# A mixture-of-experts tile loop on one core: both first-product halves of a tile in a row, then the turn, then both output halves of the preceding tile

## What is computed

```python
xf = x.reshape(-1, C)                                   # 4096 tokens, C = 256
logits = jnp.einsum('nc,ec->ne', xf, router_w)          # 8 experts
top_w, top_i = jax.lax.top_k(jax.nn.softmax(logits, axis=-1), TOP_K)
top_w = top_w / jnp.sum(top_w, axis=-1, keepdims=True)
comb = jnp.einsum('nk,nke->ne', top_w, jax.nn.one_hot(top_i, E, dtype=xf.dtype))
h = jax.nn.gelu(jnp.einsum('nc,ech->enh', xf, w1), approximate=False)   # 1024 hidden
y = jnp.einsum('enh,ehc->enc', h, w2)
out = jnp.einsum('ne,enc->nc', comb, y)
```

## Time and profile before

| what | before |
|---|---|
| runs | 735.88, 734.77 and 732.49 us, median 734.77 us |
| profiled execution | 730.98 us, span 729.1 us, mean granted clock 0.901 |
| PE busy | 616.1 us, 84% of the span |
| DVE busy | 378.1 us, 52% |
| ACT busy | 344.4 us, 47% |
| POOL busy | 264.2 us, 36% |
| chain that ended last | PE 59%, issue 15%, POOL 13%, DVE 5%, ACT 5% |

### The profile page before, as it was taken

How to read it: one execution, slowest core, us unless ns; L and a number is a source line. 1 busy time by engine, 2 the same in 40 slices (tenths; PEclk the granted TensorE clock), 3 DMA queues, 4 the chain that set the end, 5 groups by cost and what they waited for, 6 DMA issues and landing times.

```text
span 729.1 us, 19000 instructions
## 1 busy us (share of the span) xinstructions
PE 616.1 (84%) x5885; PEld 487.5 (67%) x5885; DVE 378.1 (52%) x1132; ACT 344.4 (47%) x686; POOL 264.2 (36%) x198
## 2 busy tenths in 40 slices
PE   3792855933998899889997999999989999999994
PEld 3482555622776777578766867768777778778782
DVE  1565663576338544843484348556756444444441
ACT  3353434444353745363545355645543554554551
POOL 0104371243046324632363336442646322232222
PEclk9999555555899999989998999999999999999998
DMA  9996412122143333323333311432333523223222
GB/s 297 379 355 214 146 38 88 32 91 74 45 111 80 76 59 111 82 66 67 111 68 80 70 49 32 98 80 45 97 52 85 117 47 52 45 46 52 47 31 23
DMA packets 44233, 68.14 MB, mean 93 GB/s; under 512 B 4832, under 2 KB 35808, under 8 KB 44000
## 3 DMA queue, kind: packets, MB, share of 16 engines
q1 hardware_dynamic: 30848, 49.09, 21.4%
q0 software_dynamic: 13296, 17.83, 14.8%
HBM read 44.89 MB, written 23.35 MB: 94 GB/s over the span
## 4 chain that ended last, share of the span: by engine, by line
PE 59%; issue 15%; POOL 13%; DVE 5%; ACT 5%; DMA 2%; SPq 0%; POOLq 0%; DVEq 0%; ACTq 0%
PE bank L696 13%; PE bank L682 8%; PE bank L684 7%; PE bank L683 7%; PE bank L697 7%; POOL rows L1509 5%; PE bank L506 4%; POOL hrs L1496 3%; PE bank L587 2%; POOL out L1519 2%; PE bank L644 2%; PE bank L618 2%; PE bank L572 1%; PE bank L559 1%; POOL rs L1476 1%
## 5 line engine op out<-in xcount | busy, mean ns | idle before, releaser
L682 PE MATMUL bank<-xT,wall 128*128 128x128 f16 x1136 | 213.7, 223 | 19.5 <-ACT xT L892 15.3
L684 PE MATMUL bank<-xT,wall 128*128 128x128 f16 x1136 | 214.3, 223 | 0.0
L683 PE MATMUL bank<-xT,wall 128*128 128x128 f16 x1136 | 214.0, 223 | 0.0
L696 PE MATMUL bank<-wall,ffn 128*128 x568 | 197.2, 387 | 3.0 <-DVE yo L1295 3.0
L1519 POOL DMA_INDIRECT out<-yo,dst x71 | 115.7, 1629 | 194.7 <-DVE yo L1295 114.5
L884 ACT ACTIVATE ffn<-bank 128x512 f32<-128x512 f32 x142 | 84.7, 596 | 189.1 <-PE bank L684 188.2
L682 PEld LDWEIGHTS bank<-xT,wall 128*128 x1136 | 114.4, 101 | 40.2 <-issue 27.2
L1289 DVE TENSOR_TENSOR gl<-ffn 128x512 f16<-128x512 f32 x94 | 65.0, 691 | 136.9 <-ACT ffn L884 75.1
L684 PEld LDWEIGHTS bank<-xT,wall 128*128 x1136 | 113.3, 100 | 1.2
L683 PEld LDWEIGHTS bank<-xT,wall 128*128 x1136 | 113.3, 100 | 1.0
L697 PE MATMUL bank<-wall,gl 128*128 x376 | 103.9, 276 | 0.0
(11 more groups left out here) (139 smaller groups left out, 874.9 us busy)
## 6 DMA issues: line engine op xcount, KB each, us to landing
wall<-in_w SPq DMA_DIRECT2D x15, 1024.0 KB, 11.8
xrow<-rows SPq DMA_DIRECT2D x71, 130.0 KB, 2.1
xin<-in_x SPq DMA_DIRECT2D x8, 512.0 KB, 4.5
kT<-in_ctx_t SPq DMA_DIRECT2D x8, 512.0 KB, 4.4
ctn<-in_ctx SPq DMA_DIRECT2D x8, 512.0 KB, 4.7
xres<-in_x SPq DMA_DIRECT2D x8, 512.0 KB, 5.0
out<-xres SPq DMA_DIRECT2D x8, 512.0 KB, 3.1
rows<-in_const_pad SPq DMA_DIRECT2D x9, 130.0 KB, 9.1
```

What stands on the lines that cost most here:

```text
L682: pe.matmul(o, hi, xT[i % XT][:, c, :], start=(c == 0), stop=False)
L683: pe.matmul(o, hi, xT[i % XT][:, CK + c, :], start=False, stop=False)
L684: mm = pe.matmul(o, lo, xT[i % XT][:, c, :], start=False, stop=(c == CK - 1))
L696: pe.matmul(YB[:, :], gh[q][:, m4, :], weights(i, w, 2 * D), start=(a == 0 and m4 == 0), stop=False)
```

## The change

Three engines' orders are changed, and nothing else: no instruction of a tile is added or dropped, and no buffer or wait is changed. On PE `hidden(i, 1)` follows `hidden(i, 0)` at once, ahead of the turn; `output(i-1, 1)` then follows the slot's pieces without a first-product half between; the four `values` products of slot 0 stand together behind it. On ACT `gelu(i, 1)` follows `gelu(i, 0)`, ahead of `tile_high(i+1)` and the slot's pieces. On DVE `low(i, 1)` follows `low(i, 0)`, ahead of `tile_low(i+1)` and the slot's pieces.

```diff
@@ PE, step
                     if live(i):
                         hidden(i, 0)
+                        hidden(i, 1)
                     if live(i + 1):
                         tile_turn(i + 1)
...
                     if j == 7 and f is not None:
                         gates(f)
-                    if live(i):
-                        hidden(i, 1)
-                    if j == 0 and w is not None:
-                        values(w, 0)
-                        values(w, 1)
-                        values(w, 2)
                     if live(i - 1):
                         output(i - 1, 1)
                     if j == 0 and w is not None:
-                        values(w, 3)
+                        for b in range(G):
+                            values(w, b)
@@ ACT, step
                     if live(i):
                         gelu(i, 0)
+                        gelu(i, 1)
                     if j == 1 and w is not None:
                         values(w, 2)
...
-                    if live(i):
-                        gelu(i, 1)
                     if live(i - 1):
                         weigh(i - 1)
@@ DVE, step
                     if live(i):
                         low(i, 0)
+                        low(i, 1)
                     if j == 0 and m is not None:
                         log_forget(m)
...
-                    if live(i):
-                        low(i, 1)
                     if live(i - 1):
                         weigh(i - 1)
```

## The result

The changed kernel takes 851.94 us (median of 3 runs, 848.29 to 854.79) against 734.77: a ratio of 1.160 (95% interval 1.151 to 1.168). The prediction was 834 us, range 803 to 880. The profiled execution took 851.94 us with a span of 850.1, so 121.0 us of span were added where the prediction's sum had 99.4.

A forecast was written before the change was run, and what follows sets the result against it. The prediction took TensorE's own work to bound the kernel, nearly all of a plain tile's 5.76 us. Its terms, 48.4 + 5.0 + 22.0 + 24.0 = 99.4 us, gave 830.4 on the profiled run, 834 us as median; range 803 to 880.

The forecast's parts named there:

- The chain: Plain tile: from the first output half's last matmul through gelu, difference and turned rows to the next tile's first matmul, 2.40 us.
- the idle time: Plain tile: TensorE has 1.42 us of own work against 2.40 us, so it waits 1.0 us each tile.
- The slow pair: Plain tile: after a wait both first-product blocks run at the slow, queue-refilling rate, 3.78 us instead of about 2.7.
- Rival 1: First-product pairs: the second block regains its speed, 1.34 us instead of 1.89, total 810 us; chance 0.12.
- plain stretch: Last pass, tiles 44 to 70 without attention: 7.62 us a tile against 5.76, over 26 tiles +48.4 us.
- The clock in the last pass: TensorE's granted clock should stay 1.00 there in spite of the waits.
- rival 2: Waits in every tile make the clock fall: about 905 us, 870 if half the time; chance 0.11.
- Slot 0: First of a pass's eight tile-and-attention slots: second block delays scores and values by one block, +1.9 us each pass.
- Slots 1 and 3: Attention passes: VectorE's list steps and residual addition lengthen the wait for rows, +3.1 us and 8.76 us a tile.
- slots 2 to 4: Passes 3 to 5: an existing 5.10 us wait swallows the added time, leaving +0.6 us a pass at half clock.
- Slot 7: Last slot: +0.5 us in passes 6 and 7 for a half-queued second block, nothing in passes 3 to 5.
- slots 1 to 6: Passes 6 and 7: these six tiles take 48.6 us against 39.98, +8.6 us each pass.

The follow-up runs named there:

- e3: The changed kernel with four gelu and four difference buffers instead of three, row and output buffers two instead of three: 791.3 us.
- e5: The changed kernel with VectorE's order put back as before, TensorE and ScalarE still changed: 807.5 us.
- e9: The changed kernel with ScalarE's copy of the turned rows put between the two gelus, ahead of the second: 848.2 us.
- e1: The changed kernel with ScalarE's and VectorE's orders put back, so only TensorE's order differs from the kernel before: 737.5 us, ratio 1.0055.
- e4: The changed kernel with expert 0's weights at a fixed address for every tile, so no register work between matmuls: 769.7 us.

## Why the prediction held, and where it was short

**The chain** was right step by step: 2.40 us predicted, 2.41 measured. So was the idle time, 1.0 us a tile. e3, e5 and e9 show that the three buffers and the two orders make it.

**The slow pair** was right in kind: it is slow because it follows a wait while registers are worked out (e1 and e4). Rival 1, a second block that regains its speed, did not happen: from first to last matmul the first block takes 1.83 us on average and the second 1.78 (tiles 44 to 69). The size was short. In the mean of these tiles the pair takes 3.97 us to the turn, the turn 0.25, the output half 1.19 and the chain 2.42, together 7.83. So the pair is 0.19 us longer than the 3.78 charged, the chain 0.02, and the other two are as charged (the turn of 0.31 in tile 51 is an odd one). These 0.2 us make the 5.4 of the plain stretch. In tile 51 the pair shows some single gaps of 0.1 to 0.2 us beside the beat; what makes them was not tried.

**The clock in the last pass** was right: 0.99, so rival 2 did not happen there. In the passes with attention, where the sum took the clock of before but for 0.6 us behind slot 3's wait, it moved both ways: pass 3 fell from 0.98 to 0.88, passes 6 and 7 from 1.00 to 0.95 and 0.97, pass 5 from 0.93 to 0.92, and pass 4 rose from 0.93 to 0.96. Whether the waits did this is not shown: each figure is of one execution, executions of the kernel before stood anywhere from 0.87 to 0.94 in the mean at nearly the same time, and e5, whose tiles wait too, kept 1.00 through passes 6 and 7.

**Slot 0** is the step that failed in its reason. The prediction held that the values wait for the scores anyway and charged one block, 1.9 us. It overlooked VectorE: `scores` (L1054) now stands behind the second difference too. The slot in pass 3 of the changed kernel, VectorE and then TensorE:

```profile
214.10 0.69 DVE L1284 TENSOR_TENSOR gl<-ffn 128x512 f16<-128x512 f32 x1 [0.28 <-ACT ffn L882]
...
214.79 1.28 DVE L1054 SCALAR_TENSOR_TENSOR ct<-bank,ct 128x512 f32<-128x512 f32 x2
```

```profile
216.13 4.79 PE L587 MATMUL bank<-vt,ct 128*128 128x65 f32 x24 [1.38 <-DVE ct L1054]
```

and in pass 7:

```profile
544.20 2.89 PE L587 MATMUL bank<-vt,ct 128*128 128x65 f32 x24 [1.30 <-DVE ct L1054]
```

The values wait 1.3 to 1.4 us in each pass, 6.8 us in all, where before 1.5 us was lost. In passes 3, 5 and 6 the 24 products also take 4.79, 4.65 and 3.51 us for 2.89, part of them at a granted clock of 0.50. Slot 0 grew by 3.6, 1.7, 3.5, 2.4 and 1.9 us, 13.1 in all for 9.5 charged. e5 shows that VectorE's order makes most of it: with the second difference back behind the scores the values wait 0.3 to 0.4 us, here in pass 6,

```profile
450.31 2.89 PE L587 MATMUL bank<-vt,ct 128*128 128x65 f32 x24 [0.41 <-DVE ct L1054]
```

and slot 0 is only 3.2 us longer in all than before, though the second block stands ahead of the last decay product there too. So about a third of the 1.9 us charged for that block is paid in e5, and the rest of slot 0's growth is VectorE's.

**Slots 1 and 3** were right: +3.1 to +3.9 in slot 1 for 3.1; in passes 6 and 7 slot 3 takes 8.89 and 8.99 us for 8.76, and in passes 3 to 5 its long wait swallows what slot 2 adds, as the prediction said; slots 2 to 4 came out even there, for the 1.8 us charged in the three passes.

**Slot 7** was mis-sized: 0.5 us were charged in passes 6 and 7, and 1.8 and 1.7 came. The router's steps on VectorE stand behind the second difference there, and the ranks wait for them; in e5, where they stand ahead of it again, slot 7 grew by 0.6 and 0.7. In passes 3 to 5, where nothing was charged, it changed by 2.8, -1.0 and 0.1 us; the cause of these was not followed. VectorE in pass 6, and TensorE's wait:

```profile
526.76 0.69 DVE L1284 TENSOR_TENSOR gl<-ffn 128x512 f16<-128x512 f32 x1 [2.26 <-ACT ffn L882]
527.37 0.18 DVE L1135 TENSOR_TENSOR oh<-cst,km 128x32 f32<-128x32 f32 x1
...
530.05 0.19 DVE L1159 TENSOR_TENSOR msk<-oh 128x32 f16<-128x32 f32 x1
```

```profile
530.30 0.19 PE L627 MATMUL bank<-msk,cbf 128*128 128x32 f16 x1 [1.25 <-DVE msk L1159]
```

What is left of the 7.4 us in passes 6 and 7 lies in slots 1 to 6 (10.5 and 11.0 us for 8.6). Slot 6 took 8.50 and 8.48 us where 7.7 was charged, pass 7 had been 1.1 us shorter before (38.9) than pass 6, from which both charges were taken, and the pair's missing 0.2 us a tile is part of the rest. How much of each pass is the lower clock was not told apart, since no run changed the clock alone.

So the forecast was right in its mechanism, and short by 18 us: 21.6 of terms that were charged too little or not at all, less the 0.5% by which the median of before stood above its profiled run, which the changed kernel's median does not.

## What to carry to other kernels

Where addresses are worked out in registers between matmuls, as here, slack ahead of a block is worth its idle time and the pace of the block too, so look at the time from the last operand's landing to the block's first matmul, even where no idle time shows. Before reordering one engine to make pairs, follow the copies that the next stage reads on the others: each step put ahead of them lengthens the chain by one step, and with it every piece queued behind. If a ring of buffers ties the second of a pair to work that the pair itself delays, the ring is one buffer short; here a fourth brought 851.9 us to 791.3, half of the way back.

## What the runs showed of the hardware

Three matmuls of 128 columns with registers worked out between them take 0.22 to 0.23 us, against 0.17 with fixed addresses (e4) or with a lead. The first matmul starts 0.39 us behind the end of its last operand with such registers, 0.09 without. A lead of 1.56 us carries 48 matmuls at 59 ns on average, with the last six at the slow beat (tile shown of e1; 61 in tiles 0 and 1); one of 0.52 carries only the first eight (e3). Even the kernel before, with no wait in a plain tile, pays some 20 us for the registers, 0.25 us of it in each plain tile. The granted clock of a pass moved by up to 0.10 with the same work (0.98 to 0.88 in pass 3, 0.93 to 0.96 in pass 4); what decides it was not shown.
